# Self-attention that projects tokens sorted by expert and gathers each pair's rows back

## The reference, cut to what matters

```python
vm = expert_mask(token_type_ids)[..., None]      # each token belongs to one of two experts, v or l
x = rms_norm(hidden_states, ln_in_w)
mixed = jnp.where(vm, x @ v_qkv, x @ l_qkv)      # 256 -> 768, the expert's own weights
q, k, v = jnp.split(mixed, 3, axis=-1)           # 16 heads of 16
q, k = apply_rotary(q, k, position_ids, l)
ctx = sdpa(q, k, v, causal=True)                 # 64 x 64 scores for each head
attn_out = jnp.where(vm, ctx @ v_dense, ctx @ l_dense)
hidden_states = residual + attn_out
...                                              # cross-attention, then a gated FFN, also by expert
```

## Time and profile before

| what | value |
|---|---|
| median of three runs | 2382.57 us (2380.17, 2382.57, 2382.70) |
| the profiled execution | 2377.41 us |
| its span, first to last instruction | 2375.6 us |
| its mean granted TensorE clock, share of 2.4 GHz | 0.964 |
| TensorE busy | 2214.3 us, 93% of the span |
| VectorE, ScalarE, GpSimd busy | 59%, 48%, 28% |

### The profile page before, as it was taken

One profiled execution on the slowest core, in us unless ns is written; L12 is line 12 of the kernel. 1 busy time (PEld: TensorE's weight loads), 2 busy tenths in 40 slices (PEclk: granted clock), 3 DMA queues, 4 the chain that ended last, 5 costly groups with the idle time before them and its releaser, 6 DMA issues.

```text
span 2375.6 us, 63756 instructions
## 1 busy us (share of the span) xinstructions
PE 2214.3 (93%) x24770; PEld 1803.3 (76%) x24771; DVE 1395.7 (59%) x2840; ACT 1131.5 (48%) x2617; POOL 653.6 (28%) x833
## 2 busy tenths in 40 slices
PE   8959999979969998899999969998999979989998
PEld 5638888856649997788888859887888866658998
DVE  6746666647763333666666655546666646774333
ACT  5755554437653333344444444535545426664333
POOL 2452222226642221111121110002222216652222
PEclk9979999979989999899999979998999989999999
DMA  7510000020022112100000010000000011011111
GB/s 227 80 19 16 16 16 16 16 75 25 29 81 63 60 58 91 49 2 2 2 2 2 2 37 1 0 7 15 14 16 16 16 47 51 29 39 52 57 58 42
DMA packets 78787, 85.87 MB, mean 36 GB/s; under 512 B 19939, under 2 KB 69680, under 8 KB 78416
## 3 DMA queue, kind: packets, MB, share of 16 engines
q1 hardware_dynamic: 57280, 43.64, 7.3%
q0 software_dynamic: 8368, 21.15, 2.6%
q10 hardware_dynamic: 12896, 17.64, 2.4%
HBM read 52.35 MB, written 21.40 MB: 31 GB/s over the span
## 4 chain that ended last, share of the span: by engine, by line
PE 82%; DVE 5%; ACT 3%; issue 2%; ACTq 1%; POOL 1%; DMA 0%; POOLq 0%; DVEq 0%; SPq 0%
PE ps_all L2225 3%; PE ps_all L2224 3%; PE ps_all L2223 3%; PE ps_all L1477 3%; PE ps_all L1077 3%; PE ps_all L1449 3%; PE ps_all L1000 3%; PE ps_all L1047 3%; PE ps_all L1001 3%; PE ps_all L1002 3%; PE ps_all L1061 2%; PE ps_all L2248 2%; PE ps_all L2250 2%; PE ps_all L2249 2%; PE ps_all L1093 2%; PE ps_all L2233 2%
## 5 line engine op out<-in xcount | busy, mean ns | idle before, releaser
L1242 POOL TENSOR_TENSOR s_kx<-s_qkt,const 128x512 f32<-128x512 f32 x128 | 131.6, 1048 | 437.7 <-ACT s_qkt L1172 437.7
L1600 POOL TENSOR_TENSOR c_kx<-c_qkt,const 128x512 f32<-128x512 f32 x128 | 130.6, 1037 | 111.4 <-ACT c_qkt L1543 111.2
L2223 PE MATMUL ps_all<-f_wh,f_xh 128*128 x396 | 154.3, 390 | 5.7 <-DVE f_xl L2371 5.7
L393 POOL TENSOR_TENSOR a_probs<-a_probs,a_sm 128x1024 f32<-128x1024 f32 x32 | 60.9, 1902 | 352.1 <-DVE a_sm L388 352.1
L1180 ACT ACTIVATE s_pt<-ps_all 128x512 f32<-128x512 f32 x128 | 69.7, 597 | 174.6 <-PE ps_all L1061 174.6
L2224 PE MATMUL ps_all<-f_wh,f_xl 128*128 x396 | 148.6, 375 | 0.0
L2225 PE MATMUL ps_all<-f_wl,f_xh 128*128 x396 | 148.5, 375 | 0.0
L2366 DVE SCALAR_TENSOR_TENSOR f_h<-ps_all,rstd,f_act_g 128x688 f32<-128x688 f32 x66 | 61.6, 934 | 143.3 <-PE ps_all L2225 129.6
L1944 ACT ACTIVATE self_w<-ps_all,a_q_bias 128x256 f32<-128x256 f32 x128 | 53.7, 471 | 189.7 <-PE ps_all L1788 189.7
L2248 PE MATMUL ps_all<-f_dh,f_hh 128*128 x396 | 116.9, 295 | 4.0 <-DVE f_hl L2381 4.0
L2287 ACT ACTIVATE f_act_g<-ps_all,rstd 128x688 f32<-128x688 f32 x66 | 55.2, 837 | 132.4 <-PE ps_all L2225 132.3
(11 more groups left out here) (319 smaller groups left out, 7336.1 us busy)
## 6 DMA issues: line engine op xcount, KB each, us to landing
s_v_swap<-s_v_own SPq DMA_DIRECT2D x128, 68.0 KB, 2.0
f_x_in<-x_sorted SPq DMA_DIRECT2D x66, 128.0 KB, 2.0
x_res<-x_sorted SPq DMA_DIRECT2D x66, 128.0 KB, 2.1
x_sorted<-x_res POOLq DMA_DIRECT2D x1, 4224.0 KB, 17.5
l_rows<-in_x SPq DMA_DIRECT2D x32, 128.0 KB, 5.2
x_res<-in_x SPq DMA_DIRECT2D x32, 128.0 KB, 6.2
x_res<-x_back SPq DMA_DIRECT2D x1, 3584.0 KB, 14.5
l_rows<-in_ctx SPq DMA_DIRECT2D x32, 64.0 KB, 6.1
```

The costliest lines, as they stand in the source:

```text
L1242: ins = nc.gpsimd.tensor_tensor(kx[:, p % 2, c], qkt[:, p % 2, 2 + c].rearrange("p (b k) -> p b k", b=2).unsqueeze(2) .broadcast_to([P, 2, ...
L1600: ins = nc.gpsimd.tensor_tensor(kx[:, p % 2, b], qkt[:, p % 2, 1, b * S:b * S + S].unsqueeze(1).broadcast_to([P, RH, S]), const[:, C_H8X:C ...
L2223: nc.tensor.matmul(bank, x_high, wh[:, w_at], start=(c == 0), stop=False)
```

## The change

Each expert layer's self-attention now reads sorted tiles. `x_sorted` is filled earlier: layer 0 scatters each pair when its residual is done (instead of `put_home`, which moves into self-attention 1's GpSimd loop), and the GELU FFN scatters the four pairs of each group before self-attention 3. The order of the sorted tiles is new: tiles of the two experts are mixed, ordered by their first token, so that the rows of pair p lie in the tiles 0 to p + 1.

Self-attention loads sorted tile t (three slots), transposes it once (two blocks, not normed), projects it with the weights of its one expert (6 matmuls instead of 12 for q and k, and for v; the weights are addressed by a register loaded from `off_qkv`), ScalarE evacuates both products with the norm's factor as scale into `rows` (three slots), SyncE writes these 392 KB to `qkv_sorted` in DRAM, and GpSimd gathers each pair's 392 KB back into `pair_rows` (five slots) with one indirect DMA. The rotation then reads SBUF instead of PSUM. Six tiles are projected ahead of the pair loop; the loop at p projects tile p + 6. In TensorE's loop `probs_t(p - 1)` now stands ahead of `dense(p - 2)`.

The core of the diff:

```diff
 # layer 0: TensorE counts ranks also for the first token of each tile
+nc.tensor.matmul(out_banks[1][:, D:D + PAIRS], first_b[:], vm_b[:, 0:PAIRS], start=True, stop=False)
+nc.tensor.matmul(out_banks[1][:, D:D + PAIRS], totals_b[:], upper33_b[:, 0:PAIRS], start=False, stop=True)
 # layer 0, VectorE: slots() grows from 11 to some 20 small operations at p == 2, and
+def tiles_before(k):    # at p == 4 and 5
+    nc.vector.tensor_tensor(to[:], up_to.unsqueeze(1).broadcast_to([P, PAIRS, PAIRS]),
+                            full_l[:].unsqueeze(2).broadcast_to([P, PAIRS, PAIRS]), ALU.is_le)
+def positions():        # at p == 6, for v and for l
+    nc.vector.tensor_reduce(to[:], counts[:], op=ALU.add, axis=AX.X)
+def slot_table():       # at p == 7: five small operations, the last one writes slot_i
 # layer 0, GpSimd
-        if 12 <= p:
-            put_home(p - 12)
-    for p in range(PAIRS - 10, PAIRS):
-        put_home(p)
+        if 14 <= p < 23:
+            put_sorted(2 * p - 28)
+            put_sorted(2 * p - 27)
+        if 23 <= p:
+            put_sorted(p - 5)
+    for p in range(PAIRS - 3, PAIRS):
+        put_sorted(p)
+def put_sorted(p):      # also in the GELU FFN, four after each group
+    pool.wait_ge(res_ok.handle, res_ok.at(p + 1))
+    pool.indirect_dma_start(x_sorted, bass.IndirectOffsetOnAxis(slot_i[:, p:p + 1], 0), x_tile(p), None)
 # self-attention, SyncE
+sp.wait_ge(sorted_put.handle, sorted_put.at(PAIRS))
+def load(t):
+    if t >= X_SLOTS:
+        sp.wait_ge(xt_pe.handle, xt_pe.at(t - X_SLOTS + 1))
+        sp.wait_ge(stat_ok.handle, stat_ok.at(t - X_SLOTS + 1))
+    sp.dma_start(x_in[:, t % X_SLOTS], x_sorted[t * P:t * P + P, :])
+def put(t):
+    sp.wait_ge(v_ok.handle, v_ok.at(t + 1))
+    sp.wait_ge(evac_ok.handle, evac_ok.at(t + 1))
+    ...
+    sp.dma_start(qkv_sorted[t * P:t * P + P, :], rows[:, t % ROW_SLOTS])
+def swap(p):
+    wait_pair(sp, p)
+    ...
+for t in range(X_SLOTS):
+    load(t)
+for t in range(NT + 4):
+    if is_tile(t):
+        put(t)
+    if is_tile(t + X_SLOTS):
+        load(t + X_SLOTS)
+    if has(t - 4):
+        swap(t - 4)
 # TensorE
+def project(t, out, lo, cols):
+    at = nc.tensor.value_load(off_qkv[0:1, t:t + 1], min_val=0, max_val=CH * 3 * D)
+    for c in range(CH):
+        w_at = bass.ds(at + (c * 3 * D + lo), cols)
+        high, low = (x[:, t % 2, c * P:c * P + P] for x in (xh, xl))
+        nc.tensor.matmul(out, high, wh[:, w_at], start=(c == 0), stop=False)
+        nc.tensor.matmul(out, high, wl[:, w_at], start=False, stop=False)
+        ins = nc.tensor.matmul(out, low, wh[:, w_at], start=False, stop=(c == CH - 1))
+    return ins
+    x_t(0)
+    for t in range(TILES):               # TILES = 6
+        proj_qk(t); x_t(t + 1); proj_v(t)
+    qk_t(0); qk_t(1)
     for p in range(PAIRS + 2):
+        t = p + TILES
         scores(p)
+        probs_t(p - 1)
         dense(p - 2)
-        probs_t(p - 1)
-        proj_qk(p + 2)
+        proj_qk(t)
         pv(p - 1)
-        xt_(p + 3)
-        proj_v(p + 2)
+        x_t(t + 1)
+        proj_v(t)
         out_t(p - 1)
         qk_t(p + 2)
 # ScalarE: norm() and v_copy() go; ahead of the loop
+    for t in range(TILES):
+        ...
+        x_high(t + 1); qk_rows(t); stat_(t + 2); v_rows(t)
 # and in it, after pt_copy(p - 1) and the exponentials of p
+        qk_rows(t); x_high(t + 1); stat_(t + 2); v_rows(t)
 # GpSimd: mix_() goes
+    for t in range(TILES):
+        rstd_(t + 2); gather(t - 3); put_home(t)      # put_home in layer 1 only
+    spread(0); spread(1)
     for p in range(PAIRS):
+        gather(p + 3); rstd_(p + TILES + 2); put_home(p + TILES)
         spread(p + 2)
+def gather(p):
+    for t in range(0 if p == 0 else p + 1, p + 2):
+        wait_put(pool, t)
+    if p >= PAIR_SLOTS:
+        pool.wait_ge(pv_pe.handle, pv_pe.at(p - PAIR_SLOTS + 1))
+    pool.indirect_dma_start(pair_rows[:, p % PAIR_SLOTS], None, qkv_sorted[0:(p + 2) * P],
+                            bass.IndirectOffsetOnAxis(slot_i[:, p:p + 1], 0))
 # VectorE: rope_products
-        dve.wait_ge(qk_pe.handle, qk_pe.at(p + 1))
+        wait_pair(dve, p)
-        a = ps_a[:].rearrange("p (h d) -> p h d", d=HD)
+        a = pair_rows[:, p % PAIR_SLOTS, 0:2 * D].rearrange("p (h d) -> p h d", d=HD)
```

More of the change, by code:

```diff
@@ L232, in build @@
         prod_ok = count("prod_ok")
-        v_in = [count(f"v_in{u}", 32) for u in range(3)]
+        v_in = [count(f"v_in{u}", 32) for u in range(4)]
+        xs_in = [count(f"xs_in{u}", 16) for u in range(3)]
+        qkv_put = [count(f"qkv_put{u}", 16) for u in range(4)]
+        qkv_in = [count(f"qkv_in{u}", 16) for u in range(5)]
+        cmp_ok = count("cmp_ok")
+        evac_ok = count("evac_ok")
         chigh_ok = count("chigh_ok")
@@ L817, in slots @@
[L817 to L822, removed]
@@ new lines, in proj_qk, with proj_v @@
+                    def proj_qk(t):
+                        pe.wait_ge(xlow_ok.handle, xlow_ok.at(t + 1))
+                        if evac_ok.due(t):
+                            pe.wait_ge(evac_ok.handle, evac_ok.at(t))
+                        project(t, ps_a[:], 0, 2 * D).then_inc(qk_pe.handle, 1)
+                    def proj_v(t):
+                        if v_ok.due(t):
+                            pe.wait_ge(v_ok.handle, v_ok.at(t))
+                        if res_ok.due(t - TILES - 1):
+                            pe.wait_ge(res_ok.handle, res_ok.at(t - TILES - 1))
+                        project(t, ps_b[:, 0:D], 2 * D, D).then_inc(v_pe.handle, 1)
@@ L1233, in _ @@
                     previous_done(pool)
-                    nc.gpsimd.memset(v_own[:].rearrange("p u h d -> p (u h d)"), 1.0).then_inc(cold.handle, 1)
+                    nc.gpsimd.memset(rows[:, :, 2 * D:QKV_ROW], 1.0).then_inc(cold.handle, 1)
                     def spread(p):
@@ new lines, in put_home @@
+                    def put_home(p):
+                        pool.indirect_dma_start(home_d, bass.IndirectOffsetOnAxis(slot_i[:, p:p + 1], 0),
+                                                token_i[:, p:p + 1], None).then_inc(home_put.handle, 16)
+                    rstd_(0)
+                    rstd_(1)
+                    for t in range(TILES):
+                        rstd_(t + 2)
+                        if has(t - 3):
+                            gather(t - 3)
+                        if n == 1 and has(t):
+                            put_home(t)
@@ L1263, in _ @@
                     for p in range(PAIRS):
-                        if p % G == G - 1 and has(p + G + 1) and (p + 1) // G + 1 < GROUPS:
-                            mix_((p + 1) // G + 1)
+                        if has(p + 3):
+                            gather(p + 3)
+                        if is_tile(p + TILES + 2):
+                            rstd_(p + TILES + 2)
+                        if n == 1 and has(p + TILES):
+                            put_home(p + TILES)
                         if has(p + 2):
@@ L1353, in _ @@
                             rope_sum(p + 2)
-                        if has(p + 3):
-                            x_low(p + 3)
+                        if is_tile(p + TILES + 1):
+                            x_low(p + TILES + 1)
                         if has(p - 1):
```

425 lines of the change are left out of this document (242 added, 183 removed).

## The result

The changed kernel takes 2358.9 us (median of four, 2356.8 to 2360.8) against 2382.4 for the kernel before in the same runs: a ratio of 0.990, 95% interval 0.9888 to 0.9912. It is 23.5 us faster where 76.5 were forecast; the sign was right and 2358.9 lies inside the range, but less than a third of the gain came. One of its two self-attentions did almost exactly what was forecast, the other lost.

What follows compares the result with a forecast made beforehand. TensorE was taken to bound the self-attention loops. Loops -106, prologues +10.4 and +15.1, layer 0 +4 sum to -76.5 us, a median of 2306 us; range 2265 to 2370.

Steps and rivals of the forecast that it cites:

- What bounds the loop: Self-attention loop: TensorE's work falls from 10.18 to 7.8 us, the period to 8.4 with some 0.6 waiting for VectorE's rope_sum.
- rival (b): Loop: two register loads of 0.3 us each before the projections stall TensorE; one mechanism of a new stall, 2358 us, chance 0.15.
- Rival (a): Loop: rotation reading two SBUF operands waits for a GpSimd operation, up to 1.05 us; mechanism of a new stall, chance 0.15.
- The clock rival: Loop: TensorE's waits lower its clock, 6.2 us more per iteration, 2616 us if in all; chance 0.05.
- the stall rival: Loop: a new stall of about 1 us per iteration, 50 x 1.05 = 52 us, total 2358; chance 0.15.
- The price of the moved step: Home scatter in self-attention 1: priced as GpSimd time, 0.30 beside the gather's 0.96 at the start, another 1.26 per iteration.
- the rival on transfers: Loop: 1.05 MB per iteration takes 4.2 us of 8.4; only past 9.9 us is all gained lost, 2385; chance 0.04.
- The order: TensorE's loop: setting probs_t ahead of dense moves no work and gains nothing by itself.
- from pair 30 on: End of each self-attention: nothing was projected there before either, so the change was left at nothing.
- The prologue: Ahead of the pair loop: six tiles in rounds of 4.9 us paced by the load; +10.4 in layer 1, +15.1 in layer 3.
- Layer 0: VectorE gets 8 us of added comparisons, reductions and small operations, of which idle time absorbs 3.7: +4 us (1 to 8).

Runs made afterwards that it cites:

- e10_wide_home: Changed kernel with each home scatter writing 128 rows of 512 bytes instead of 4-byte words, at the same place in self-attention 1: 2300.5 us, ratio 0.966.
- e2_home_both: Changed kernel with the home scatters issued a second time, same values, in self-attention 3 at the same places as in self-attention 1: 2447.8 us.
- e6_home_cross: Changed kernel with the home scatters moved from self-attention 1 into cross-attention 1's GpSimd loop, one per iteration: 2353.0 us.
- e12_wide_dense: e10_wide_home with TensorE's order undone, dense(p - 2) again ahead of probs_t(p - 1): 2315.9 us, 15.3 above.
- e8_cross_five: e6_home_cross with five tiles instead of six projected ahead of the pair loop: 2348.0 us.

## Why the prediction was right in one layer and wrong in the other

**What bounds the loop: the number right, the wait not.** Layer 3's period is 8.29, forecast 8.4. But the forecast had 7.8 us of TensorE's work and a wait of 0.6 for VectorE's last step (rope_sum). TensorE is busy for 8.10, and its waits for that step are 1.7 us in all, four times in the loop. The chain that ended last through one iteration of layer 3 names TensorE and one gap (the last line is rope_sum, from VectorE's timeline):

```profile
1748.24 0.92 PE ps_all L1167 x16
1749.16 1.02 PE ps_all L1181 x8
...
1752.95 1.05 PE ps_all L1199 x64
1754.01 0.37 PE ps_all L1114 x2
1754.38 0.19 issue
1754.56 0.38 PE ps_all L1122
...
1755.54 0.22 PE ps_all L1206 x2
1755.76 0.44 PE ps_all L1149 x4
...
1754.71 0.68 DVE L1431 TENSOR_TENSOR s_roped<-s_roped 128x512 f32<-128x512 f32 x1
```

rope_sum ends at 1755.39, but qk_t (L1149) starts at 1755.76: behind pv, x_t, the gap, proj_v and out_t fill 1.75 us, more than VectorE needs (1.38). So two errors cancel, and that the period came out is luck in part: the wait of 0.6 isn't there, and 0.3 us of work and a gap of 0.19 are that were not forecast.

The gap of 0.19 stands ahead of proj_v, where the weight offset is loaded: of rival (b)'s stall some 0.2 of an iteration came (5.3 us in 25 iterations of layer 3, first fence of waits). Rival (a) did not come in the loop: the rotation, with two SBUF operands, takes 0.68 where the earlier trace rows had 0.69 from PSUM, and GpSimd's spread never runs beside it there. At layer 3's start it came once, with the price that the forecast gave it: pair 1's rotation runs beside pair 0's spread, and its last two instructions take 1.29 and 1.42 us instead of 0.42 and 0.68.

```profile
1654.47 2.26 POOL L1356 TENSOR_TENSOR pool_w<-s_qkt,const 128x512 f32<-128x512 f32 x2
1654.53 1.29 DVE L1426 TENSOR_TENSOR s_roped<-pool_w,rope 128x256 f32<-128x256 f32 x1
1655.86 1.42 DVE L1431 TENSOR_TENSOR s_roped<-s_roped 128x512 f32<-128x512 f32 x1
```

The clock rival did not come: the granted clock is 1.00 in layer 3's iterations. That the whole took 2358.9, within 1 us of the 2358 that the stall rival named, is chance.

**The price of the moved step: this is the step that failed.** "gather and home scatter at 0.96 + 0.30 each" and, in the loop, "in layer 1 another 1.26: 5.4 of 8.4" price the home scatter by its GpSimd time alone. Its DMA stands in no term, without a reason given, and the rival on transfers counted an iteration's kilobytes, among which 512 bytes vanish. In layer 0 it had slowed the loads beside it, but no step there waited for a DMA. In the new loop a load, a put and a gather are due in each iteration. The same scatter costs 48 us there and 15 to 18 ahead of it (after against e10_wide_home, and e2_home_both's layer 3), and 56 in cross-attention 1 (e6_home_cross against the other kernels with the change). With the pieces made wider the prediction's sum stands: forecast 2306, measured 2300.5. By stage its loops (-52.1 and -53.1) and starts (+8.6 and +14.1) are met; that two terms left at nothing cancel, -9.8 us behind pair 30 and +9 in the stages that the change doesn't touch, is luck. The Trainium skill (DMA: Bandwidth & Descriptors, section "Specifications") says that under 512 bytes the DMA engine does a read-modify-write. The words of 4 bytes (landing in some 7 us instead of 2.6) agree with a penalty of that kind; the rows of 64 bytes don't: they landed in 2.4 to 2.6. The measurement decides: here only the single words hurt.

**The order: wrong.** "it gains nothing by itself" looked at the steady iteration only, where it holds to 0.05 us. Where no projections are left the order decides what covers ScalarE's copy, and it is worth 15 us (e12_wide_dense). The forecast's "from pair 30 on ... I leave that at nothing" is the term: 5.9 and 4.6 us measured.

**The prologue: right in layer 3, for other reasons.** +13.9 for +15.1. But its rounds are 3.8 to 3.9 us (the fifth is 4.9), not 4.9, and the load doesn't set them. The v_rows of tiles 0 and 1 in the timeline of after, TensorE's wait in these rounds, and the busy time over one of them:

```profile
1631.97 0.47 ACT L1280 ACTIVATE pool_w<-ps_all,s_factor 128x256 f32<-128x256 f32 x1
...
1635.87 0.45 ACT L1280 ACTIVATE pool_w<-ps_all,s_factor 128x256 f32<-128x256 f32 x1
...
PE ps_all L1122 <- ACT pool_w L1275: 4.7, 4, 1.2
...
1635.90:1639.70 3.80, 2.58 (x14) 2.07 (x14) 1.72 (x3) 2.85 (x9) 0.74 (x2) 1.00 0.43 140
```

In a round TensorE works 2.58 us, with a granted clock of 1.00, and waits 1.2 for ScalarE's copy of q and k out of PSUM (L1275), which stands behind the next tile's split; the tile is there in time. (The expectation for e8_cross_five took these rounds for matmuls at the low clock. Only the first tile's are, at a granted clock of 0.50.) What was forecast too dear there was forecast too cheap at both ends: v_rows(0) after 13.0 us instead of 12.4, and 6.1 instead of 4 from the last v_rows to the scores, of which 1.6 are rival (a)'s. In layer 1 the rounds were 5.2, 6.2, 6.6, 7.3 and 8.2, with one home scatter issued in each. There the load does set them: ScalarE waits 19.2 us for it in four of them.

**Layer 0: right**, +2.3 for +4.

**What stays open.** Cross-attentions and FFNs, which the change doesn't touch, are 8 us longer in sum (9 in e10_wide_home); their steady stretches have the clock 1.00 in both kernels, and the last 20 us of the cross-attentions a lower one after than before (0.77 and 0.87 against 0.97 and 1.00). Why was not tried. Nor do the runs show what a 4-byte word does in the DMA engines, only that it lands late, and that gathers, loads and instructions beside it get slow.

## What to carry to other kernels

Price a moved DMA where it goes, not where it stood: ask what else is on the DMA engines there and who waits for it, and count its pieces, not its bytes. That nothing waits where it stands now doesn't make it cheap: look there at how long the DMAs beside it take to land. A scatter of single words cost 48 us in one loop; the same number in a row of 512 bytes cost that loop nothing. And test an order of instructions at the ends of a loop too: what covers a copy in the steady state is gone in the last iterations.

## What the hardware showed

- An indirect scatter of 128 words of 4 bytes, side by side in DRAM, landed some 7 us after its issue (5.5 to 8.9, layer 0 of the kernel before); rows of 64 and of 512 bytes landed in 2.4 to 2.7. Its own packets took 0.014 us each.
- What is queued beside it pays: in self-attention 1 the gathers' packets took 1.32 us instead of 0.33, the instruction packets 3.1 instead of 1.0, and one 128 KB load 12.3 us, where such loads landed in 2.6 (median) with the scatters in another stage; in layer 0 of the kernel before a 128 KB load took 5.6 instead of 2.1.
- While these scatters stand in it, a loop's time differs between kernels in which it is the same code: 296.5, 305.6, 307.3 us.
- 1.05 us of GpSimd work in an iteration (a memset) cost nothing in a loop of 8.29 us.
- VectorE instructions with two SBUF inputs took 1.29 and 1.42 us instead of 0.42 and 0.68 while GpSimd multiplied in SBUF, and 1.27 and 1.26 instead of 0.42 in e10_wide_home. At no other place in these two kernels did the two run beside each other.
